# One-hot rows of the odd tiles moved to GpSimd, between its gathers, in a graph attention kernel

## The reference

```
xl = x @ Wl + bl
e_feat = leaky_relu(xl[src] + (x @ Wr + br)[dst], 0.2)
logits = einsum('ehc,hc->eh', e_feat, att)
m = segment_max(logits, dst);  a = exp(logits - m[dst])
a = a / segment_sum(a, dst)[dst]
out = segment_sum(xl[src] * a[:, :, None], dst)
```

## Time and profile before

| | before |
|---|---|
| median of 3 runs | 8319.16 us (8298.82 to 8323.32) |
| the profiled execution's own time | 8224.01 us |
| its span | 8221.9 us |
| mean granted clock of TensorE | 0.703 of full speed |
| GpSimd busy | 4777.4 us (58%), 4843 instructions |
| TensorE busy | 5220.3 us (63%) |
| VectorE busy | 4814.5 us (59%) |
| ScalarE busy | 4364.0 us (53%) |
| queue of the gathers (software) | 154752 packets, 327.15 MB, 17.8% of 16 engines |
| queue of the other DMAs (hardware) | 247917 packets, 217.13 MB, 9.5% |

### The profile page before, as it was taken

One profiled execution on the slowest core, in us unless ns is written; L12 is line 12 of the kernel. 1 busy time (PEld: TensorE's weight loads), 2 busy tenths in 40 slices (PEclk: granted clock), 3 DMA queues, 4 the chain that ended last, 5 costly groups with the idle time before them and its releaser, 6 DMA issues.

```text
span 8221.9 us, 103854 instructions
## 1 busy us (share of the span) xinstructions
PE 5220.3 (63%) x25358; PEld 4292.5 (52%) x25358; DVE 4814.5 (59%) x13989; ACT 4364.0 (53%) x10671; POOL 4777.4 (58%) x4843
## 2 busy tenths in 40 slices
PE   5676676777766755665666666666565665566656
PEld 2666666666656444554555555434444554445444
DVE  3555555555555655655666656655666665666656
ACT  2555455555555455555555555545555555555546
POOL 1666666666666166666666666616666666666640
PEclk7777777777777666666666666656666666666666
DMA  4333323333333422222222222242222222222221
GB/s 122 85 85 84 84 79 84 86 85 84 85 85 85 88 54 53 54 53 54 55 54 54 54 54 54 54 86 54 54 54 54 54 54 54 54 54 54 54 53 47
DMA packets 402713, 544.76 MB, mean 66 GB/s; under 512 B 124846, under 2 KB 310244, under 8 KB 394734
## 3 DMA queue, kind: packets, MB, share of 16 engines
q0 software_dynamic: 154752, 327.15, 17.8%
q1 hardware_dynamic: 247917, 217.13, 9.5%
HBM read 490.62 MB, written 53.26 MB: 66 GB/s over the span
## 4 chain that ended last, share of the span: by engine, by line
POOL 50%; issue 32%; DMA 10%; PE 4%; DVE 2%; ACT 1%; POOLq 1%; SPq 0%; DVEq 0%; ACTq 0%
POOL xl_g L643 50%; DMA xl_g<-xl_tab,edges 9%; PE PS L676 2%; PE PS L795 1%; PE PS L675 1%; DVE ea L1071 0%; PE PS L729 0%; POOLq L638 0%; POOLq L641 0%; ACT n_hT L831 0%; DMA state<-n_new 0%; ACT msg L950 0%; DMA digit_tab<-S 0%; DMA ea<-state 0%; POOLq L633 0%
## 5 line engine op out<-in xcount | busy, mean ns | idle before, releaser
L643 POOL DMA_INDIRECT xl_g<-xl_tab,edges x4836 | 4776.6, 988 | 3184.8 <-issue 2738.8
L1140 DVE TENSOR_TENSOR z<-PS,xl_g 128x528 f32<-128x528 f32 x1302 | 868.8, 667 | 2786.2 <-DMA xl_g<-xl_tab,edges 2226.0
L729 PE MATMUL PS<-msg,S 128*128 128x137 f32 x9672 | 1844.6, 360 | 1011.3 <-DVE msg L1239 772.6
L729 PEld LDWEIGHTS PS<-msg,S 128*128 128x128 f32 x9672 | 1680.5, 256 | 1173.9 <-issue 1059.5
L703 PE MATMUL PS<-xr_w,ST 128*128 128x132 f32 x9672 | 1929.7, 360 | 61.5 <-DVE z L1140 44.5
L875 ACT ACTIVATE distT<-PS,neg_node 128x512 f32<-128x512 f32 x1302 | 843.1, 648 | 1934.3 <-PE PS L693 787.7
L703 PEld LDWEIGHTS PS<-xr_w,ST 128*128 128x128 f32 x9672 | 1747.2, 265 | 200.5 <-issue 170.3
L852 ACT ACTIVATE dist<-node_row,neg_dst 128x128 f32<-128x128 f32 x4836 | 1534.6, 386 | 0.0
L693 PE MATMUL PS<-digits,digit_w 2*128 2x512 bf16 x1302 | 598.0, 459 | 1276.7 <-ACT distT L875 794.0
L693 PEld LDWEIGHTS PS<-digits,digit_w 2*128 2x128 bf16 x1302 | 122.6, 94 | 1570.4 <-ACT distT L875 907.8
L1147 DVE SCALAR_TENSOR_TENSOR am<-z,att_relu 128x512 f32<-128x512 f32 x1302 | 854.8, 657 | 6.4
(11 more groups left out here) (200 smaller groups left out, 3278.6 us busy)
## 6 DMA issues: line engine op xcount, KB each, us to landing
xl_g<-xl_tab,edges POOLq DMA_INDIRECT x4836
ea<-edge_attr SPq DMA_DIRECT2D x62, 1248.0 KB
xr_w<-xr_tab SPq DMA_DIRECT2D x186, 66.0 KB
dst_r<-dst_rows SPq DMA_DIRECT2D x186, 64.0 KB
node_row<-node_id SPq DMA_DIRECT2D x186, 64.0 KB
xl_tab<-xl_g SPq DMA_DIRECT2D x30, 330.0 KB, 3.7
xr_tab<-xl_g SPq DMA_DIRECT2D x30, 330.0 KB, 5.2
st_old<-state SPq DMA_DIRECT2D x124, 68.0 KB
```

The lines of the kernel that those rows point to most:

```text
L643: pool.indirect_dma_start(xl_g[:, q, t, :], None, xl_tab[:, :], bass.IndirectOffsetOnAxis(idx[:, q, t:t + 1], 0))\
L729: last = pe.matmul(agg_ps, S[:, q, t, :], msg[:, t, :], start=t == 0, stop=t == TILES - 1)
L1140: dve.tensor_tensor(out=z[:, (q + g) % 2, 0:n, :], in0=zp[(q + g) % 2][:, 0:n, :], in1=xl_g[:, q, a:a + n, :], op=ALU.add).then_inc(z_done ...
```

## The change

GpSimd makes the one-hot rows of the odd tiles, each with one `tensor_scalar` (add, then is_equal to 0) of 128x128 straight into `S`. ScalarE makes those of the even tiles, in the old way, half as many per group. An odd tile is made after the gather of an even tile: during the second half of an item's gathers (tiles 14 to 24) the item's tiles 1 to 11, and during the first half of the next item's (tiles 0 to 12) its tiles 13 to 25.

GpSimd no longer waits for the group before to land. It waits, ahead of group g, for all tiles of group g - 2 (for the first two groups that is a group of the item before). `most_gathered` is gone, and `gathered` has one semaphore for each group, of all its tiles. After tile 13 GpSimd waits for the item's `neg_dst` and for the sums of the item two before. TensorE waits for the odd tiles that a group of sums needs, and SyncE for the item's last odd tile before it loads the item two ahead. The cuts of the attribute sums in stage 0 go over five groups instead of four. The first pair of items of a stage stands outside the loop, and the last item's odd tiles from 13 on are made behind the loop.

```diff
--- before.py
+++ after.py
@@ -47,7 +47,8 @@
 GROUPS = [range(a, min(a + 4, TILES)) for a in range(0, TILES, 4)]
 NG = len(GROUPS)
 SUMS_AT = {2: (0,), 3: (1, 2), 4: (3, 4), 5: (5, 6)}
-EA_CUTS = (0, 4, 9, 16, TILES)
+EA_CUTS = (0, 6, 12, 17, 21, TILES)
+HALF = TILES // 2
 LH = TILES * HEADS
 SQ = 32
 LP = SQ * HEADS
@@ -295,8 +296,8 @@
         ea_loaded = sems("ea_loaded", 2)
         state_loaded = sems("state_loaded", 2)
         state_stored = sem("state_stored")
-        most_gathered = sems("most_gathered", NG - 1)
-        gathered = [sems(f"gathered{q}_", NG) for q in range(2)]
+        gathered = sems("gathered", NG)
+        odd_onehot = sem("odd_onehot")
         spacer = sem("spacer")
         negdst_done = sem("negdst_done")
         flag_done = sems("flag_done", 5)
@@ -572,6 +573,8 @@
                         sp.sem_inc(spacer, 1)
                         sp.wait_ge(logit_done[NG - 1], (before + k + 1) * 3)
                         sp.sem_inc(spacer, 1)
+                        sp.wait_ge(odd_onehot, (before + k + 1) * HALF)
+                        sp.sem_inc(spacer, 1)
                         load_item(k + 2, q)
                         sp.wait_ge(item_done, before + k + 1)
                         sp.dma_start(here, st_new[:, q, 0:width]).then_inc(state_stored, 16)
@@ -630,25 +633,51 @@
                 for q in range(2):
                     pool.wait_ge(n_stored[q], stored_value * ((stage + 1) * (ROUNDS // 2) + 1))
                 pool.sem_inc(spacer, 1)
-                with pool.Fori(0, pairs) as i:
+
+                def item_gathers(i, q, first):
+                    v = pairs * (2 * stage) + 2 * i + (q + 1)
+
+                    def odd_tile(of, k, t):
+                        pool.tensor_scalar(S[:, of, t, :], node_row[:, of, :], neg_dst[:, of, t:t + 1], 0.0, ALU.add, ALU.is_equal).then_inc(odd_onehot, 1)
+
+                    pool.wait_ge(idx_loaded[q], (pairs * stage + i + 1) * 16)
+                    for g, tiles in enumerate(GROUPS):
+                        pool.wait_ge(msg_done[g], v)
+                        pool.sem_inc(spacer, 1)
+                        if g >= 2:
+                            pool.wait_ge(gathered[g - 2], v * (16 * len(GROUPS[g - 2])))
+                            pool.sem_inc(spacer, 1)
+                        elif stage or not first:
+                            pool.wait_ge(gathered[g - 2], (v - 1) * (16 * len(GROUPS[g - 2])))
+                            pool.sem_inc(spacer, 1)
+                        for t in tiles:
+                            pool.indirect_dma_start(xl_g[:, q, t, :], None, xl_tab[:, :],
+                                                    bass.IndirectOffsetOnAxis(idx[:, q, t:t + 1], 0))\
+                                .then_inc(gathered[g], 16)
+                            if t < HALF and t % 2 == 0 and not first:
+                                odd_tile(1 - q, v - 1, HALF + t)
+                            if t == HALF:
+                                pool.wait_ge(negdst_done, v)
+                                pool.sem_inc(spacer, 1)
+                                pool.wait_ge(agg_done, v)
+                                pool.sem_inc(spacer, 1)
+                            if t > HALF and t % 2 == 0:
+                                odd_tile(q, v, t - HALF)
+
+                item_gathers(0, 0, True)
+                item_gathers(0, 1, False)
+                with pool.Fori(1, pairs) as i:
                     for q in range(2):
-                        pool.wait_ge(idx_loaded[q], (pairs * stage + i + 1) * 16)
-                        for g, tiles in enumerate(GROUPS):
-                            pool.wait_ge(msg_done[g], pairs * (2 * stage) + 2 * i + (q + 1))
-                            pool.sem_inc(spacer, 1)
-                            if g:
-                                pool.wait_ge(most_gathered[g - 1], (pairs * (2 * stage) + 2 * i + (q + 1)) * (16 * (len(GROUPS[g - 1]) - 1)))
-                                pool.sem_inc(spacer, 1)
-                            for t in tiles:
-                                pool.indirect_dma_start(xl_g[:, q, t, :], None, xl_tab[:, :],
-                                                        bass.IndirectOffsetOnAxis(idx[:, q, t:t + 1], 0))\
-                                    .then_inc(gathered[q][g] if g == NG - 1 or t == tiles[-1] else most_gathered[g], 16)
+                        item_gathers(i, q, False)
+                for t in range(HALF, TILES, 2):
+                    pool.tensor_scalar(S[:, 1, t, :], node_row[:, 1, :], neg_dst[:, 1, t:t + 1], 0.0, ALU.add, ALU.is_equal).then_inc(odd_onehot, 1)
 
         @block.tensor
         def _(pe):
 
             for g in range(NG):
                 pe.sem_inc(msg_done[g], 2)
+            pe.sem_inc(agg_done, 2)
             pe.wait_ge(ones_made, 1)
             pe.wait_ge(setup, SETUP_ROW_STEPS)
             pe.matmul(flat[:, 0:2 * N_CHUNKS], ones[0:1, :], tab_row[:, :, :].rearrange("a w c -> a (w c)"),
@@ -718,6 +747,7 @@
                             pe.wait_ge(ea_loaded[q], use * 16)
                             pe.wait_ge(onehot_done[NG - 1], v * 2)
                             pe.wait_ge(runs_done, v)
+                        pe.wait_ge(odd_onehot, v * HALF + ((tiles[-1] + 1) // 2 - HALF))
                         for t in tiles:
                             pe.matmul(ea_ps, S[:, q, t, :], ea[:, q, t, :], start=t == 0, stop=t == TILES - 1)
 
@@ -725,6 +755,7 @@
                         q, v, use = closes
                         pe.wait_ge(onehot_done[g], v * 2)
                         pe.wait_ge(msg_done[g], v + 2)
+                        pe.wait_ge(odd_onehot, v * HALF + ((GROUPS[g][-1] + 1) // 2 - HALF))
                         for t in GROUPS[g]:
                             last = pe.matmul(agg_ps, S[:, q, t, :], msg[:, t, :], start=t == 0, stop=t == TILES - 1)
                         if g == NG - 1:
@@ -844,15 +875,15 @@
                     def onehot(g):
 
                         q, v, use = opens
-                        n = len(GROUPS[g])
+                        n = len(GROUPS[g]) // 2
                         if g == 0:
                             act.wait_ge(item_loaded[q], use * (16 * ITEM_DMAS))
                             act.wait_ge(negdst_done, v)
-                        for m, t in enumerate(GROUPS[g]):
+                        for m, t in enumerate(GROUPS[g][::2]):
                             last = act.activation(dist[:, (q + g) % 2, m, :], node_row[:, q, :], ACT.Abs, bias=neg_dst[:, q, t:t + 1])
                         last.then_inc(onehot_done[g], 1)
                         act.wait_ge(onehot_done[g], v * 2 - 1)
-                        act.activation(S[:, q, GROUPS[g][0]:GROUPS[g][0] + n, :], dist[:, (q + g) % 2, 0:n, :], ACT.Relu, bias=1.0, scale=-1.0)\
+                        act.activation(S[:, q, GROUPS[g][0]:GROUPS[g][0] + 2 * n:2, :], dist[:, (q + g) % 2, 0:n, :], ACT.Relu, bias=1.0, scale=-1.0)\
                             .then_inc(onehot_done[g], 1)
 
                     def penalties():
@@ -1133,10 +1164,7 @@
                     q, v, use = opens
                     a, n = GROUPS[g][0], len(GROUPS[g])
                     dve.wait_ge(expanded[g], v)
-                    if g < NG - 1:
-                        dve.wait_ge(most_gathered[g], v * (16 * (n - 1)))
-                        dve.sem_inc(spacer, 1)
-                    dve.wait_ge(gathered[q][g], use * (16 if g < NG - 1 else 16 * n))
+                    dve.wait_ge(gathered[g], v * (16 * n))
                     dve.tensor_tensor(out=z[:, (q + g) % 2, 0:n, :], in0=zp[(q + g) % 2][:, 0:n, :], in1=xl_g[:, q, a:a + n, :],
                                       op=ALU.add).then_inc(z_done[g], 1)
 
@@ -1244,7 +1272,7 @@
                 def new_max():
 
                     q, v, use = closes
-                    dve.wait_ge(agg_done, v)
+                    dve.wait_ge(agg_done, v + 2)
                     dve.tensor_scalar(some[:, :], agg_ps[:, M_ONE:M_MAX], 1.0, None, ALU.min).then_inc(merge_step, 1)
                     dve.wait_ge(merge_step, v * 4 - 3)
                     dve.tensor_scalar(none_pen[:, :], some[:, :], -1.0, BIG, ALU.add, ALU.mult).then_inc(merge_step, 1)
```

## The result

The changed kernel takes 8785.95 us (median of four runs, 8777.49 to 8793.39) beside 8308.99 us for the kernel before in the same measurement: ratio 1.0574, 95% interval 1.0549 to 1.0599. The prediction was 8027 us, faster, with a range up to 8480. The result is slower and outside the range. The profiled execution took 8793.39 us, with a span of 8791.6.

What follows compares the result with a forecast made beforehand. GpSimd's gathers and the idle time before them were taken as the bound. From 8224.0 us, less 1259 for pauses, plus 967 for added instructions, came 7932; with 95 carried over, 8027 us, range 7600 to 8480.

Steps and rivals of the forecast that it cites:

- What bounds the kernel: Whole kernel: GpSimd's gathers and the idle time before them fill 7961 of the span's 8222 us.
- The pauses: GpSimd at group changes: 1278 us of idle time waiting for landings, of which removal gains 1259 us.
- another engine isn't the bound: Edge stages: an item would take 38 us, while TensorE, the busiest other engine, has 29 in stage 0.
- The added instruction, c: Cost of each of 2418 one-hot instructions on GpSimd, put at 0.40 us, 967 us in all.
- break-even of 0.52: Cost in us per added GpSimd instruction at which the change neither gains nor loses time.
- Meeting VectorE: Added GpSimd instructions wait for VectorE instructions with two SBUF inputs: 0.08 us each on average.
- Dispatch: Start cost of each added GpSimd instruction, 0.03 us, from the start distance of narrow memsets.
- the dear instruction: Rival: each added GpSimd instruction costs over 0.52 us; with its own 0.305 idle, 0.70, giving 8750 us; chance 22%.
- nearly-free rival: Added instruction fits into the idle 0.30 us behind each gather, costing 0.10 us: 7300 us; chance 8%.
- The new waits: Added waits on GpSimd, TensorE, SyncE and VectorE's merged wait: claimed to cost nothing.
- What would show it: Stage 1 gather starts 1.65 us apart across an added instruction, otherwise 1.25; item 38.9; GpSimd busy about 5670, ScalarE about 3200.
- The range: Whole kernel: 7600 to 8480 us, for added-instruction costs of 0.22 to 0.59 us, with two in ten outside.

Runs made afterwards that it cites:

- e1: Kernel before with only the new waits (group g waits for group g-2), nothing added on GpSimd: 10240.11 us, ratio 1.2426.
- e8: Kernel before with the new waits alone, plus a one-column memset behind the last gather of each group: 10273.18 us, ratio 1.2404.
- e2: Odd tiles' one-hot rows on GpSimd as in the change, but with the waits of the kernel before: 9069.99 us, ratio 1.0998.
- e4: Changed kernel with the comparison left out of the added instruction, one operation instead of two: 8602.78 us, ratio 1.0437.
- e5: Changed kernel with each added instruction split into two of 64 columns: 9518.63 us, ratio 1.1488.
- e15: Changed kernel with the constant -5.0 in place of the per-partition scalar in the added instructions: 8709.52 us beside 8255.07, one run.
- e12: Kernel before with the new waits alone, plus a one-column memset per group on whose completion GpSimd waits: 8105.86 us, ratio 0.9799.
- e6: Changed kernel with each added instruction replaced by a memset of the same 128x128 rows: 8824.74 us, ratio 1.0643.
- e10: Kernel before with the new waits alone, plus a 384-column memset per group on which GpSimd waits: 8651.38 us, ratio 1.0531.
- e9: Kernel before with the new waits alone, plus a 768-column memset per group on which GpSimd waits: 8925.05 us, ratio 1.0863.

## Why the prediction was wrong, point by point

- **What bounds the kernel**: right. GpSimd's order of gathers set the end before and sets it after.
- **The pauses**: right in the changed kernel, where none is left. Wrong as a term that stands by itself: alone their removal costs 24% instead of bringing 1259 us. That this did not show in the changed kernel, where 2% of TensorE's completions are late, is luck, since the prediction had no term for it. What failed there is the sentence that another engine isn't the bound because TensorE has only 29 us of work in an item of 38. TensorE's busy time was right (it is lower still in e1), but its completions reach the others late when gathers follow each other at 1.25 us. No row that I showed named this, though the waits of the kernel before have 524 and 436 us on "remote", which I did not follow.
- **The added instruction, c**: the step that failed, and the one that explains the result. c was put at 0.40 us and came out at 0.76, over the break-even of 0.52. I took 0.29 from affine_select; the instruction measured 0.73. Both read, compare and write 128x128, but what a GpSimd operation costs per column does not carry over from one kind to another. Meeting VectorE was right: 0.08 taken, 0.09 by the mean over the median. Dispatch (0.03 added) was wrong in the cheap direction: the idle 0.30 behind a gather takes in an instruction, and it costs some 0.1 us less than its length. 0.64 for the distance and 0.09 for the longer gather behind it, with the remainder in meetings, make 0.76.
- **The rivals**: the dear instruction gave 8750 us, within 0.5% of the result, for a false reason. It set a further 0.305 on an instruction of 0.29; there is no such gap. The nearly-free rival had the true mechanism (the memset run: 0.22 us for 0.08) and the wrong length.
- **The new waits**: right for GpSimd and SyncE. TensorE does wait for odd tiles, 401.6 us in the view of its waits, where I had put it at nothing; it does cost next to nothing, since line 760 holds 0% of the chain.
- **What would show it**: pairs at 1.65 and 1.25 forecast, 1.89 and 1.34 measured; item 38.9 and 43.4; GpSimd busy 5670 and 6865; ScalarE about 3200 and 3422. "Over 0.52 and the forecast falls" was the right test.
- **The range**: its upper end, c = 0.59, was set by chances and not by a row; with c up to 0.98 as my own upper bound it was too narrow.

## What to carry to other kernels

Where an engine's order of work sets the end, price an instruction that is put into it by the same operation on the same engine, or measure it first; a neighbour of the same shape was off by a factor of 2.5 here. Before a pause is taken out, look for waits that no recorded instruction ends, since something else may get through in it. And a fixed pause can be cheaper than one that waits for data: 1.1 us per four gathers was worth 2.0%.

## What the runs showed of the hardware that was not expected

- With indirect DMAs issued at 1.25 us without a pause, semaphores raised by matmuls come up to 24 us and more after the recorded end (e1); those of VectorE and ScalarE are on time. In e8 under 1% are late up to the third gather behind a long stop, and 98% from the fifth on.
- It was absent (0 of some 9700 in three kernels) where GpSimd waited for an instruction of its own and 2.37 us or more lay between the starts. That wait is not needed: in the changed kernel, e2, e4, e5 and e15, which have none, 0.5 to 2% are late, with an instruction of 0.62 us or more (or two of 0.5) behind every second gather and 1.77 us or more across it. Nor does it suffice: with the wait and 2.06 us per group (e12) 38% are late. A memset of 0.22 us behind every second gather (e6: 1.33 us) leaves 43%. More free time between the gathers goes with less lateness, but it is not the whole of it: the kernel before, with 2.0 to 2.4 us at the group changes, has 38%, and e10 with 2.37 has none. The mechanism is open: the runs show what goes with lateness, not what path is held up, and none shows whether it would be there without the profile's recording. The records of 0 to 29% of the rises are missing, and what they would have shown is not known. That lateness makes e1 slow is argued from the "remote" waits and from e9 and e10, which differ from e1 only in the memset and its wait.
- A GpSimd instruction behind an indirect DMA starts in the 0.30 us that otherwise pass idle: 0.12 us cost nothing, 0.22 cost 0.08.
- GpSimd's wait for its own completion costs 1.0 us from the instruction's end to the next gather, beside 0.17 to 0.30 without it.
